# Cross-attention and mixed-basis FFN: the first tile multiplies float32 weights as they land

## What is computed

```python
probs = jax.nn.softmax(xt @ w_router, axis=-1)            # 512 x 128
topk_p, topk_idx = jax.lax.top_k(probs, 4)
gate = (xt @ w_gate).reshape(T, 8, 256)                   # 512 x 2048
up = (xt @ w_up).reshape(T, 8, 256)                       # 512 x 2048
basis = jax.nn.silu(gate) * up
...
mixed = jnp.einsum('tek,tki->tei', mix_sel, basis)
down = jnp.einsum('tei,ih->teh', mixed, w_down)
...
shared = jax.nn.silu(xt @ shared_w_gate) * (xt @ shared_w_up) @ shared_w_down
...
x = x + _L0_xattn_ref(_layernorm(x, axis=-1), ctx_2048)
x = x + _L0_ffn_ref(_layernorm(x, axis=-1), ...)
```

## Time and profile before

| what | us |
|---|---|
| median of the 3 runs | 636.28 |
| lowest and highest run | 633.89, 636.39 |
| the profiled execution's own time | 634.54 |
| its span, first to last instruction | 632.8 |
| TensorE busy in the span | 538.8 (85%) |
| VectorE, ScalarE, GpSimd busy | 395.9, 240.7, 199.6 |

### The profile page before, as it was taken

One profiled execution on the slowest core, in us unless ns is written; L12 is line 12 of the kernel. 1 busy time (PEld: TensorE's weight loads), 2 busy tenths in 40 slices (PEclk: granted clock), 3 DMA queues, 4 the chain that ended last, 5 costly groups with the idle time before them and its releaser, 6 DMA issues.

```text
span 632.8 us, 7958 instructions
## 1 busy us (share of the span) xinstructions
PE 538.8 (85%) x2637; PEld 252.7 (40%) x2637; DVE 395.9 (63%) x1133; ACT 240.7 (38%) x340; POOL 199.6 (32%) x242
## 2 busy tenths in 40 slices
PE   1306636599989999999999999999999999999993
PEld 0103213244444444444454444444444444444441
DVE  6946576477867747685857476767565656563311
ACT  5366537544334333334344342342524242423110
POOL 3301021303835131654441413563514141411110
PEclk9999657699999999999999999999999999999997
DMA  8512530211211232021212311111212121111101
GB/s 284 181 67 66 167 133 0 83 26 35 50 34 34 50 97 55 25 60 25 51 34 50 101 42 42 40 44 26 59 25 60 26 58 26 41 26 35 25 18 41
DMA packets 61753, 37.10 MB, mean 59 GB/s; under 512 B 49168, under 2 KB 49680, under 8 KB 61712
## 3 DMA queue, kind: packets, MB, share of 16 engines
q1 hardware_dynamic: 61712, 36.59, 21.4%
HBM read 20.72 MB, written 4.19 MB: 39 GB/s over the span
## 4 chain that ended last, share of the span: by engine, by line
PE 72%; DVE 11%; ACT 8%; issue 6%; POOL 1%; DMA 1%; SPq 0%; POOLq 0%; DVEq 0%; ACTq 0%
PE gate L906 30%; PE up L906 27%; PE even L936 10%; DVE x L1136 3%; PE odd L888 2%; ACT gate_up_hi L600 2%; ACT gate_up_hi L613 2%; DVE gate_up_lo L1303 1%; ACT L659 1%; DVE ctx_m L1058 1%; PE even L860 1%; PE odd L860 1%; DMA ctx_in<-in_ctx 1%; ACT L663 1%; PE turn L826 1%
## 5 line engine op out<-in xcount | busy, mean ns | idle before, releaser
L675 ACT ACTIVATE silu<-gate,w_back 128x512 f32<-128x512 f32 x80 | 55.0, 688 | 194.9 <-PE gate L906 194.7
L906 PE MATMUL gate<-gate_up_hi,zT_hi 128*128 128x512 f16 x320 | 124.9, 390 | 0.0
L906 PE MATMUL gate<-gate_up_lo,zT_hi 128*128 128x512 f16 x320 | 124.7, 390 | 0.0
L906 PE MATMUL gate<-gate_up_hi,zT_lo 128*128 128x512 f16 x320 | 124.2, 388 | 0.0
L906 PE MATMUL up<-gate_up_hi,zT_hi 128*128 128x512 f16 x320 | 121.3, 379 | 0.0
L906 PE MATMUL up<-gate_up_lo,zT_hi 128*128 128x512 f16 x320 | 121.3, 379 | 0.0
L906 PE MATMUL up<-gate_up_hi,zT_lo 128*128 128x512 f16 x320 | 121.3, 379 | 0.0
L1232 DVE SCALAR_TENSOR_TENSOR part<-up,coef,silu 128x256 f32<-128x256 f32 x128 | 55.9, 478 | 54.2 <-PE up L906 53.9
L547 POOL TENSOR_TENSOR hid<-hid,part 128x256 f32<-128x256 f32 x48 | 34.8, 725 | 162.9 <-DVE part L1232 162.7
L531 POOL TENSOR_TENSOR gain<-var,minus_half 128x1 f32<-128x1 f32 x16 | 11.3, 703 | 138.9 <-DVE neg_mean L1150 138.9
L906 PEld LDWEIGHTS gate<-gate_up_hi,zT_lo 128*128 128x128 f16 x320 | 32.0, 100 | 40.1 <-issue 4.1
(11 more groups left out here) (156 smaller groups left out, 824.8 us busy)
## 6 DMA issues: line engine op xcount, KB each, us to landing
ctx_in<-in_ctx SPq DMA_DIRECT2D x16, 256.0 KB, 3.7
x_in<-in_x SPq DMA_DIRECT2D x16, 256.0 KB, 2.9
out<-y_out SPq DMA_DIRECT2D x16, 256.0 KB, 2.2
stage<-in_L_ffn_w_up SPq DMA_DIRECT2D x3, 1024.0 KB, 5.1
stage<-in_L_ffn_w_gate SPq DMA_DIRECT2D x2, 1024.0 KB, 8.2
ctx_in<-in_L_ffn_w_gate SPq DMA_DIRECT2D x2, 1024.0 KB, 5.1
stage<-in_L_ffn_shared_w_gate SPq DMA_DIRECT2D x1, 1024.0 KB, 7.5
stage<-in_L_ffn_shared_w_up SPq DMA_DIRECT2D x1, 1024.0 KB, 9.8
```

The lines of the kernel that those rows point to most:

```text
L675: nc.scalar.activation(silu[:, k % 2, :], gate_ps[k % 2][:], ACT.Silu, scale=w_back[:, n:n + 1]).then_inc(silu_done, 1)
L906: mm = nc.tensor.matmul(ps[:], zT[a][:, t % 2, kc, :], wgu[w][:, n - 1 + i, kc, :], start=(m == 0), stop=(m == 3 * KC - 1))
```

## The change

Tile 0 no longer uses split weights. `norm2(0)` makes only `y2`; TensorE transposes it in float32 (`turn_z32`), ScalarE copies it into `z32T` (a part of `y_out`), and `route32` and `pair32` multiply it with the float32 chunks where they were staged, one float32 matmul in place of three float16 ones. A staging place may only be loaded again after the chunk is split and tile 0 has multiplied it (`wait_first_tile`). Two more places are parts of the split weights' own memory, those of chunks 9 and 10 (`LENT`), which is why `wgu` is now one tensor. The splits are still made, beside tile 0, for tile 1: those of chunks `DOWN`, 9 and 10 now fall into tile 1. In tile 0 the weights need no scale, so `w_back` falls away there, and with it `unscale_coef`. The router and chunks 1 and 2 now share one scale group.

```diff
-    GROUPS = [(0, 1)] + [(n, min(n + 2, CHUNKS)) for n in range(1, CHUNKS, 2)]
+    GROUPS = [(0, 3)] + [(n, min(n + 2, CHUNKS)) for n in range(3, CHUNKS, 2)]
...
-    SLOT = {1: 0, 2: 1, 3: 2, 4: 3, 5: 4, 6: 0, 7: 1, 8: 2, 9: 4, 10: 0, DOWN: 3}
+    SLOT = {1: 0, 2: 1, 3: 2, 4: 3, 5: 5, 6: 6, 7: 4, 8: 0, 9: 1, 10: 2, DOWN: 3}
+    ORDER = list(range(9)) + [DOWN, 9, 10]
+    LENT = {9: 5, 10: 6}
...
                 if slot_before(n):
                     wait_ready(sp, slot_before(n))
+                    wait_first_tile(sp, slot_before(n))
...
+            def keep_z32():
+                act.wait_ge(turned0, turn_of(HI, "z", 0) + 1)
+                nc.scalar.copy(z32T.rearrange("p c n -> p (c n)"), turn_ps[0][:]).then_inc(kept0, 1)
...
+            def turn_z32():
+                pe.wait_ge(y2_done, 1)
+                bank_free(HI, "z", 0)
+                for kc in range(KC):
+                    mm = nc.tensor.transpose(turn_ps[0][:, kc * P:(kc + 1) * P], y2[:, kc * P:(kc + 1) * P], ident32[:])
+                mm.then_inc(turned0, 1)
...
+            def pair32(p, between={}):
...
+                k, n = use(0, p), chunk(p)
+                for i, (ps, full) in enumerate(((gate_ps[k % 2], gate_full), (up_ps[k % 2], up_full))):
+                    for kc in range(KC):
+                        if KC * i + kc in between:
+                            between[KC * i + kc]()
+                        if kc == 0:
+                            pe.wait_ge(kept0, turn_of(HI, "z", 0) + 1)
+                            wait_staged(pe, n + i)
+                            wait_at(pe, (silu_done, up_read)[i], k - 1)
+                        mm = nc.tensor.matmul(ps[:], z32T[:, kc, :], w_staged(n + i)[:, kc * CW:(kc + 1) * CW],
+                                              start=(kc == 0), stop=(kc == KC - 1))
+                    mm.then_inc(full, 1)
...
+            turn_z32()
+            route32()
+            pair32(-1, {1: lambda: flip_w(1), 4: lambda: spread_w(1), 6: lambda: [turn_x(1), attend(1, 0)]})
+            pair32(0, {2: lambda: [attend(1, 1), flip_w(2)], 4: lambda: spread_w(2), 5: lambda: attend(1, 2),
+                       7: lambda: [turn_weight(0), attend(1, 3)]})
+            pair32(1, {2: lambda: coefs(0), 5: lambda: flip_w(3), 7: lambda: spread_w(3)})
+            pair32(2, {5: lambda: [turn_z(1, HI), turn_z(1, LO)]})
+            pair32(3, {0: lambda: route(1), 1: lambda: flip_w(4), 4: lambda: spread_w(4), 5: lambda: flip_w(5)})
             spread_w(5)
...
             turn_weight(1)
-            pair(0, 3)
```

More of the change, by code:

```diff
@@ L223, in build @@
         side = slice(SIDE, SIDE + P)
-        stage_in = [sem(f"stage_in{i}") for i in range(5)]
+        stage_in = [sem(f"stage_in{i}") for i in range(7)]
         router_in, small_in = sem("router_in"), sem("small_in")
@@ L344, in wait_ready @@
         def wait_ready(eng, n):
[L345 removed]
+            eng.wait_ge(w_ready, ORDER.index(n) + 1)
         def wait_staged(eng, n):
@@ L558, in _ @@
             round_x(1)
-            for t in range(TILES):
+            rstd_of(2)
+            rstd2_of(1)
+            mix_parts(0, 0)
+            round_x(2)
+            mix_parts(0, 1)
+            mix_parts(0, 2)
+            for t in range(1, TILES):
                 b = t // NB
@@ L690, in _ @@
             norm1(0)
+            scale_ctx(2)
             sum_w(0)
-            scale_ctx(2)
+            sum_w(1)
+            sum_w(2)
+            keep_ctx(0)
             scale_ctx(3)
-            sum_w(1)
-            for c in range(2):
-                keep_ctx(c)
+            sum_w(3)
+            keep_ctx(1)
+            keep_ctx(2)
             keep_x(0)
-            for c in range(2, NB):
-                keep_ctx(c)
+            keep_ctx(3)
             split_w(0)
-            sum_w(2)
             split_w(1)
-            split_w(2)
             norm1(1)
-            sum_w(3)
             sum_w(4)
             norm2(0)
-            keep_z(0)
+            split_w(2)
+            keep_z32()
+            sum_w(5)
+            sum_w(6)
+            silus(0, -1)
+            keep_x(1)
+            exps(0)
             split_w(3)
+            sum_w(7)
             split_w(4)
-            exps(0)
-            sum_w(5)
-            silus(0, -1)
+            keep_weight(0)
             abs_shared(0)
-            sum_w(6)
-            keep_weight(0)
-            keep_x(1)
             split_w(5)
+            sum_w(8)
             silus(0, 0)
+            norm1(2)
+            norm2(1)
             split_w(6)
-            sum_w(7)
-            sum_w(8)
-            norm2(1)
             split_w(7)
+            keep_z(1)
             silus(0, 1)
-            split_w(8)
-            sum_w(9)
-            keep_z(1)
-            sum_w(10)
-            norm1(2)
-            split_w(9)
-            silus(0, 2)
-            split_w(10)
-            exps(1)
-            sum_w(DOWN)
+            sum_w(9)
+            silus(0, 2)
+            sum_w(10)
+            sum_w(DOWN)
+            exps(1)
+            split_w(8)
+            keep_weight(1)
             silus(0, 3)
             split_w(DOWN)
-            keep_weight(1)
             for t in range(1, TILES):
@@ L1349, in _ @@
-            mixes()
+            quantise_x(1)
             lo_w(1)
-            z_lo(ln, 0)
+            lane_chain = lane_w(1)
+            top_chain = largest(0)
+            scales_w(lane_chain, 1)
+            keep_up_back(0)
+            stats(2)
             lo_w(2)
-            scale_of_w(2)
-            quantise_x(1)
-            pick(largest(0), 0)
+            attention(1, 0)
+            pick(top_chain, 0)
+            attention(1, 1)
+            lane_chain = lane_w(2)
             combine(0, -1)
+            scales_w(lane_chain, 2)
@@ L1367, in _ @@
             lo_w(6)
-            scale_of_w(4)
-            unscale_coef(1)
+            combine(0, 1)
+            quantise_x(2)
             lo_w(7)
-            combine(0, 1)
-            lo_w(8)
-            stats(2)
-            scale_of_w(5)
-            unscale_coef(2)
-            top_chain = largest(1)
-            lo_w(9)
-            quantise_x(2)
-            lo_w(10)
-            combine(0, 2)
-            scale_of_w(6)
-            unscale_coef(3)
-            pick(top_chain, 1)
-            lo_w(DOWN)
+            lane_chain = lane_w(4)
@@ L1386, in _ @@
+            top_chain = largest(1)
+            scales_w(lane_chain, 4)
+            keep_up_back(3)
+            combine(0, 2)
+            lane_chain = lane_w(5)
+            scales_w(lane_chain, 5)
+            pick(top_chain, 1)
+            lo_w(8)
             for t in range(1, TILES):
@@ L1397, in _ @@
                 split_h(hid_chain, s)
+                if t == 1:
+                    lo_w(DOWN)
                 if front:
@@ L1400, in _ @@
                 combine(t, -1)
+                if t == 1:
+                    lo_w(9)
                 if b > 0:
```

170 lines of the change are left out of this document (86 added, 84 removed).

## The result

The changed kernel takes 601.97 us (median of four runs, 601.66 to 602.66) against 635.83 for the kernel before, run beside it (633.89 to 636.39). The ratio is 0.9474, with a 95% interval of 0.9451 to 0.9497. Repeated in a later comparison it was 602.27 us and 0.9471 (0.9446 to 0.9497). The forecast was 601. The profiled execution of the changed kernel has a span of 600.9 us, that of the kernel before 632.8.

The account below looks back on a forecast made before the run. TensorE's pace in tiles 2 to 15 and tile 1's start bound the kernel. Tile 1 41.2 us earlier, less 6.8 of waits, starts tile 2 at 128.6 instead of 163.0: 34.4 us less, forecast 601, range 594 to 613.

Parts of the forecast that it names:

- The start of tile 0's products: Tile 0: `route32` starts at 39.1 us, 14 us earlier than 53.16, and the pairs start at 40.9.
- My walk: Tiles 0 and 1: the four engine lists followed with profiled durations to find start times and waits.
- The price of a float32 multiplication: Tile 0's products, 512 columns: four passes at 2.4 GHz, 0.86 us, bounded between 0.43 and 1.72 us.
- Rival 2: Tile 0: a float32 multiplication costs 0.43 us, so TensorE is 17 us shorter; time 595 us, chance 0.06.
- Tile 0's sum: Tile 0 on TensorE: 40.9 + 35.3 + 6.9 + 4.3 + 1.6 = 89.0 us, where tile 1 starts instead of 130.2.
- Tile 1: Three moved low halves make TensorE wait 6.8 us: tile 1 lasts 39.6 us, tile 2 starts at 128.6.
- the third wait: Tile 1: TensorE's `flip_ctx(1)` waits 2.7 us behind `lo_w(10)` and `max_ctx` on VectorE.
- rival 3: Tile 0: the clock stays at 1.2 GHz, tile 1 starts at about 120; time 632 us, chance 0.07.
- Tile 2 on: From tile 2 to the end: nothing changes, same list and shapes, 470 us as before.
- Rival 1: Mainly tile 1: VectorE is later than walked, disturbed by GpSimd, costing 5 to 12 us; 607 to 613, chance 0.14.
- Rival 4: Tile 0: float32 weight loads wholly exposed at 1.2 GHz, 27 us on top of rival 3; 659 us, chance 0.03.
- The cover of the loads: Tile 0: chunk loads cost nothing, hidden by tile 0 itself; without that cover each would show about 5 us.

Follow-up runs that it names:

- Short low halves: Changed kernel with the low halves of the down weights and chunks 9 and 10 cut to 16 columns on VectorE, zeros elsewhere: 595.47 us, ratio 0.9368.
- the filled wait: Changed kernel with 13 unused 16-bit multiplications added in TensorE's 3.08 us wait ahead of `flip_ctx(1)` in tile 1: 601.30 us, ratio 0.9455.

## Why the prediction was right

- **The start of tile 0's products.** `route32` at 39.1, measured 38.83; the pairs at 40.9, measured 40.69. My walk had `y2` done at 36.7, and it is done at 36.4 (35.60 and 0.81). The order of `mixes` ahead of attention cost 0.13 us (28.57 to 28.70), not 0.45.
- **The price of a float32 multiplication**, the term on which the most hung: 0.86 us from two rows of other shapes, measured 0.86. The Trainium skill, "FP8 and Floating Point Precision" (TensorE Precision Notes), has four passes, and the trace agrees: 0.86 us against 0.215 for a float16 multiplication. Where the Trainium skill, "Perfetto Trace Analysis" (Engine Utilization), halves the rate for FP32_LOW_HIGH, that holds for each record here, and there are two of them: the whole is a quarter of the rate. Rival 2 with its 0.43 us a multiplication fell by the step. Its reckoning, that a cheaper product gives back only some 6 us, held: with a single pass, half the price of the rival, the time was 596.5 against its 595.
- **Tile 0's sum.** 89.0, measured 89.03, but with errors that cancel, so the hundredths are luck: five profiles with the same tile 0 have 87.74 to 89.28. The clock rose after nearly five records of `pair32` in this execution, not after one multiplication: some 1.2 us more on the products. The waits were 0.90 (as forecast), 1.49 for 2.2, 1.74 for 1.2, 0.97 for 1.6 at `pick(1)`, and 0.25 for a scale that I had not listed: 5.35 for 5.9. The pairs began 0.2 sooner, and the small work on TensorE took the last half microsecond less than I gave it. Where the engine that waits comes later the wait is shorter, so an error on TensorE's side moves the sum less than its own size.
- **Tile 1.** The waits were forecast as 1.6, 2.5 and 2.7, 6.8 in all, and are 1.45, 2.31 and 3.08, 6.84 in all. Short low halves take all three away. The single ones are off by 0.15, 0.19 and 0.38 us, and their sum agrees by luck.
- **The step that failed**: "Tile 1 lasts 32.8 + 6.8 = 39.6 us". It lasted 41.35. The missing 1.7 us are the stretch at 1.2 GHz behind the third wait, shown by the filled wait, which brings it to 39.67. I had let the clock stay at the full level in tile 1 and written in rival 3 that TensorE has no gap over 2.5 us; that was tile 0, and in tile 1 my own walk had one of 2.7.
- **Tile 2 on**: 470 us, measured 470.5. The profile of before was of a span of 632.8, and its own sum gives 598.4 for the span after; the measured 600.9 is 2.5 more, 1.8 of it the slow stretch and 0.7 behind tile 2.
- **The rivals.** Rival 1 (VectorE later than walked) did not come: its low halves kept 2.34 and 3.41 us. Two roundings of x on GpSimd took 3.3 us (at 37.62 and 77.79), but no wait of TensorE in tiles 0 and 1 ended on GpSimd. Rival 3 fell by the steps, 0.43 us from 45 us on, with the granted clock at 1.00 there too; the 1.00 from 40.7 to 44.8 us is no evidence, for the steps are 0.85 there. Rival 4 needed the weight loads to show; the 80 records of `pair32` follow each other at 0.43 us wherever nothing else stands between them, with 15.0 us of their loads beside 39.5 of matmul.
- **The cover of the loads.** I said the cover was tile 0 itself and each load 5 us if it were gone. Without the two places it was 21.6 us in all, since ScalarE's list holds the sums in order and TensorE's small work stands behind them. As long as the places were there the walk held: chunks 7 to 10 and the down weights were issued at 30.3, 46.6, 51.8, 60.9 and 68.4 us, against 31, 46, 51, 60 and 68.

## What to carry to other kernels

Where splitting a weight into halves keeps the first tile waiting, a full-precision product of four passes can be the cheaper one, as long as it comes once and the split is made beside it: tile 1 came 41 us sooner here, and a product of a single pass would have added only 5 to 6. The buffers that let the raw data lie until it is used belong to that change: alone they gave nothing, and without them two thirds of the gain were lost. Work that leaves a critical stretch is paid where it lands; walk the lists of that stretch too, and count a wait of three microseconds on TensorE as nearly five, unless TensorE has to wait for another engine soon behind it: there the slow stretch cost nothing.
